# Gated cross-attention and FFN on one core: TensorE's blocks in another order, with the other engines' orders fitted to it

## The reference

```python
x = x + jnp.tanh(g_xattn[0]) * _L0_xattn_ref(_layernorm(x), ctx_1024, mask, Wq, bq, Wk, bk, Wo, bo)
x = x + jnp.tanh(g_ffn[0]) * _L0_ffn_ref(_layernorm(x), weights, scale, bias)

# _L0_xattn_ref, one head
Q = query @ Wq.T + bq;  K = ctx @ Wk.T + bk
attn = softmax(where(mask, -inf, Q @ K^T));  out = (attn @ ctx) @ Wo.T + bo
# _L0_ffn_ref
y = clip((x @ (2 * (weights >= 0) - 1).T) * scale + bias, -100, 100)
```

## Time and profile before

| | us |
|---|---|
| median of 3 runs | 83.87 (83.54 to 83.89) |
| the profiled execution | 83.47 |
| its span, first to last instruction | 81.3 |
| busy in the span: TensorE | 69.5 (85%) |
| VectorE, GpSimd | 55.1, 54.9 (68% each) |
| ScalarE | 36.5 (45%) |

### The profile page before, as it was taken

How to read it: one execution, slowest core, us unless ns; L and a number is a source line. 1 busy time by engine, 2 the same in 40 slices (tenths; PEclk the granted TensorE clock), 3 DMA queues, 4 the chain that set the end, 5 groups by cost and what they waited for, 6 DMA issues and landing times.

```text
span 81.3 us, 1571 instructions
## 1 busy us (share of the span) xinstructions
PE 69.5 (85%) x524; PEld 65.2 (80%) x524; DVE 55.1 (68%) x162; ACT 36.5 (45%) x98; POOL 54.9 (68%) x102
## 2 busy tenths in 40 slices
PE   2999899979999999999999999999999898905000
PEld 2998797967899999999999999999999797704000
DVE  2394823995369589939957962894697468972980
ACT  0052538736476519436751943585094436020000
POOL 6006557503898508889999998999998995149900
PEclk9999999999999999999999999999999999998555
DMA  1999999960000000030003003000300300300051
GB/s 16 274 371 353 349 347 348 348 186 0 0 4 0 0 0 8 0 133 0 0 23 110 8 0 129 0 0 0 129 8 0 129 0 0 129 0 0 0 194 65
DMA packets 7713, 7.44 MB, mean 92 GB/s; under 512 B 791, under 2 KB 7450, under 8 KB 7706
## 3 DMA queue, kind: packets, MB, share of 16 engines
q1 hardware_dynamic: 7376, 7.34, 28.0%
q10 hardware_dynamic: 330, 0.01, 0.2%
HBM read 5.25 MB, written 2.10 MB: 90 GB/s over the span
## 4 chain that ended last, share of the span: by engine, by line
PE 73%; DVE 14%; ACT 5%; issue 2%; POOL 2%; POOLq 0%; DVEq 0%; ACTq 0%
PE ps_K L514 16%; PE ps_Z L514 13%; PE ps_S L578 8%; PE ps_O L597 8%; PE ps_F L514 7%; PE ps_x1T L616 6%; PE ps_cT L509 4%; PE ps_xT L509 4%; PE ps_x1T L509 4%; ACT K_sb L205 2%; PE ps_S L586 2%; DVE cT_lo L372 2%; DVE out_sb L425 2%; DVE f_last L422 1%; DVE f_scaled L417 1%
## 5 line engine op out<-in xcount | busy, mean ns | idle before, releaser
L397 DVE SCALAR_TENSOR_TENSOR x_sb<-ps_O,recip_p,xb_sb 128x256 f32<-128x256 f32 x16 | 7.0, 479 | 10.4 <-PE ps_O L597 10.3
L314 POOL TENSOR_TENSOR f_biased<-f_scaled,bi_g 128x256 f32<-128x256 f32 x14 | 10.0, 735 | 3.8 <-DVE f_scaled L405 3.7
L308 POOL TENSOR_TENSOR xb_sb<-x_sb,bo_g 128x256 f32<-128x256 f32 x16 | 11.4, 733 | 0.5 <-ACT bo_g L241 0.5
L514 PE MATMUL ps_F<-wT,x1T_hi 128*128 128x256 f32 x32 | 8.6, 303 | 2.4 <-DVE f_scaled L405 2.3
L195 ACT CAST cT_hi<-ps_cT 128x512 fp32r<-128x512 f32 x8 | 4.7, 586 | 13.3 <-PE ps_cT L509 13.2
L296 POOL TENSOR_SCALAR xn<-x_sb,rstd_x,off_x 128x256 f32<-128x256 f32 x16 | 9.8, 621 | 0.5
L514 PE MATMUL ps_K<-cT_hi,wqk_hi 128*128 128x256 f32 x32 | 9.3, 290 | 0.9 <-DVE cT_lo L372 0.9
L514 PE MATMUL ps_Z<-woT_hi,cT_hi 128*128 128x256 f32 x32 | 9.7, 304 | 0.0
L514 PE MATMUL ps_K<-cT_hi,wqk_lo 128*128 128x256 f32 x32 | 9.0, 282 | 0.0
L514 PE MATMUL ps_K<-cT_lo,wqk_hi 128*128 128x256 f32 x32 | 9.0, 281 | 0.0
L514 PE MATMUL ps_Z<-woT_lo,cT_hi 128*128 128x256 f32 x32 | 9.0, 280 | 0.0
(11 more groups left out here) (102 smaller groups left out, 195.0 us busy)
## 6 DMA issues: line engine op xcount, KB each, us to landing
x_sb<-in_x_dram SPq DMA_DIRECT2D x8, 256.0 KB, 5.9
ctx_sb<-in_ctx_dram SPq DMA_DIRECT2D x8, 256.0 KB, 6.1
out_dram<-out_sb SPq DMA_DIRECT2D x7, 256.0 KB, 2.1
wq_sb<-in_L_xattn_Wq_dram SPq DMA_DIRECT2D x1, 256.0 KB, 3.1
wk_sb<-in_L_xattn_Wk_dram SPq DMA_DIRECT2D x1, 256.0 KB, 3.4
wo_sb<-in_L_xattn_Wo_dram SPq DMA_DIRECT2D x1, 256.0 KB, 4.5
w_sb<-in_L_ffn_weights_dram SPq DMA_DIRECT2D x1, 256.0 KB, 4.9
out_dram<-out_sb SPq DMA_DIRECT2D x2, 128.0 KB, 1.9
```

The costliest lines, as they stand in the source:

```text
L308: nc.gpsimd.tensor_tensor(xb_sb[:, r], x_sb[:, r], bo_g[:], ALU.add).then_inc(xb_done, 1)
L314: nc.gpsimd.tensor_tensor(f_biased[:, r], f_scaled[:, r], bi_g[:], ALU.add).then_inc(f_biased_done, 1)
L397: nc.vector.scalar_tensor_tensor(out=x1_sb[:, r], in0=ps_O[:, b], scalar=recip_p[:, r:r + 1], in1=xb_sb[:, r], op0=ALU.mult, op1=ALU.add). ...
L514: last = nc.tensor.matmul(dst, lhsT, rhs, start=(n == 0), stop=(n == len(pairs) - 1))
```

## The change

TensorE's loop becomes, for iteration i: Z(i), K(i+1), ffn(i-1), P^T(i), transposes of ctx(i+2) and x(i+2), O(i), scores(i+1), transposes of x1(i). scores(0) and the transposes of group 1 stand ahead of the loop. The orders on ScalarE, VectorE and GpSimd change with it, and the second unit of four rows of x is cut in two units of two. No computation is added or taken away, except that GpSimd computes one more unit's offsets (four small instructions).

```diff
--- before.py
+++ after.py
@@ -40,9 +40,9 @@
     row = lambda v: v.rearrange("(o d) -> o d", o=1)
 
 
-    UNITS = [(0, 2), (2, 4), (4, 8), (8, 12), (12, 16)]
-
-    STATS_AT = {0: (2, 3), 1: (4, 5), 2: (6,), 3: (7,)}
+    UNITS = [(0, 2), (2, 4), (4, 6), (6, 8), (8, 12), (12, 16)]
+
+    STATS_AT = {1: (4, 5), 2: (6,), 3: (7,)}
     unit_of = lambda g: next(n for n, (lo, hi) in enumerate(UNITS) if lo <= g * GB < hi)
 
     with ExitStack() as stack:
@@ -239,26 +239,31 @@
             nc.scalar.activation(woT_hi[:], ps_woT, ACT.Identity, scale=tanh_g[:, 0:1]).then_inc(woT_hi_ready, 1)
             act.wait_ge(ps_bo_ready, 1)
             nc.scalar.activation(bo_g[:], x1T_bank[:, 0:D], ACT.Identity, scale=tanh_g[:, 0:1]).then_inc(bo_g_ready, 1)
+            evict_cT_hi(1)
+            exp(0)
+            evict_xT(1)
             for i in range(G - 1):
-                evict_cT_hi(i + 1)
-                exp(i)
                 if i >= 1:
                     evict_x1T_hi(i - 1)
-                evict_xT(i + 1)
+                    exp(i)
                 evict_Z(i)
-                evict_PT(i)
                 evict_K(i + 1)
                 if i == 0:
                     act.wait_ge(ps_wT_ready, 1)
                     nc.scalar.copy(wT[:], ps_x1T).then_inc(wT_ready, 1)
+                evict_PT(i)
+                if i + 2 < G:
+                    evict_cT_hi(i + 2)
+                    evict_xT(i + 2)
+                if i == 0:
                     act.wait_ge(ps_rows_ready, 1)
                     nc.scalar.activation(sc_g[:], f_bank[:, 0:D], ACT.Identity, scale=tanh_g[:, 1:2]).then_inc(sc_g_ready, 1)
                     nc.scalar.activation(bi_g[:], f_bank[:, D:2 * D], ACT.Identity, scale=tanh_g[:, 1:2]
                                          ).then_inc(bi_g_ready, 1)
             exp(G - 1)
+            evict_x1T_hi(G - 2)
             evict_Z(G - 1)
             evict_PT(G - 1)
-            evict_x1T_hi(G - 2)
             evict_x1T_hi(G - 1)
 
         @block.gpsimd
@@ -325,21 +330,20 @@
             norm_x(1)
             pool.wait_ge(bo_g_ready, 1)
             for i in range(G):
-                add_bo(i)
-                if i == 2:
-                    pool.wait_ge(bi_g_ready, 1)
-                    pool.wait_ge(clip_ready, 2)
-                if i >= 2:
-                    bias_and_clip(i - 2)
+                if i >= 1:
+                    rstd_1s(i - 1)
                 if i + 2 < G:
                     if unit_of(i + 2) != unit_of(i + 1):
                         offsets_x(unit_of(i + 2))
                     norm_x(i + 2)
+                add_bo(i)
+                if i == 1:
+                    pool.wait_ge(bi_g_ready, 1)
+                    pool.wait_ge(clip_ready, 2)
                 if i >= 1:
-                    rstd_1s(i - 1)
-
+                    bias_and_clip(i - 1)
             rstd_1s(G - 1)
-            bias_and_clip(G - 2)
+
             for b in range(GB):
                 r = (G - 2) * GB + b
                 pool.wait_ge(f_clip_done, G - 1)
@@ -462,42 +466,38 @@
             dve.wait_ge(abs_g_done, 1)
             nc.vector.tensor_scalar(clip_hi[:], abs_g[:], CLIP, None, ALU.mult).then_inc(clip_ready, 1)
             nc.vector.tensor_scalar(clip_lo[:], abs_g[:], -CLIP, None, ALU.mult).then_inc(clip_ready, 1)
-            for i in range(G - 1):
-                if i >= 1:
-                    residual(i - 1)
-                max_of_scores(i)
-                if i >= 2:
-                    scale_ffn_out(i - 2)
-                if i == 0:
-                    dve.wait_ge(w_loaded, 16)
-                    nc.vector.tensor_scalar(w_sign2[:], w_sb[:], 0.0, 2.0, ALU.is_ge, ALU.mult).then_inc(sign2_done, 1)
-                    dve.wait_ge(sign2_done, 1)
-                    nc.vector.tensor_reduce(w_sum[:], w_sign2[:], AX.X, ALU.add).then_inc(w_sum_done, 1)
-                split_cT(i + 1)
-                if i == 0:
-                    dve.wait_ge(w_sum_done, 1)
-                    nc.vector.tensor_scalar(w_mean[:], w_sum[:], 1.0 / D, None, ALU.mult).then_inc(w_mean_done, 1)
-                    dve.wait_ge(w_mean_done, 1)
-                    for c in range(DC):
-                        nc.vector.tensor_scalar(w_cent[:, c], w_sign2[:, c], w_mean[:, c:c + 1], None, ALU.subtract
-                                                ).then_inc(w_cent_ready, 1)
+            max_of_scores(0)
+            split_cT(1)
+            stats_x(2)
+            dve.wait_ge(w_loaded, 16)
+            nc.vector.tensor_scalar(w_sign2[:], w_sb[:], 0.0, 2.0, ALU.is_ge, ALU.mult).then_inc(sign2_done, 1)
+            dve.wait_ge(sign2_done, 1)
+            nc.vector.tensor_reduce(w_sum[:], w_sign2[:], AX.X, ALU.add).then_inc(w_sum_done, 1)
+            dve.wait_ge(w_sum_done, 1)
+            nc.vector.tensor_scalar(w_mean[:], w_sum[:], 1.0 / D, None, ALU.mult).then_inc(w_mean_done, 1)
+            dve.wait_ge(w_mean_done, 1)
+            for c in range(DC):
+                nc.vector.tensor_scalar(w_cent[:, c], w_sign2[:, c], w_mean[:, c:c + 1], None, ALU.subtract
+                                        ).then_inc(w_cent_ready, 1)
+            stats_x(3)
+            for i in range(G):
                 if i >= 1:
                     stats_x1(i - 1)
                     split_x1T(i - 1)
+                if i >= 2:
+                    final(i - 2)
                 for g in STATS_AT.get(i, ()):
                     stats_x(g)
-                if i >= 2:
-                    final(i - 2)
-            scale_ffn_out(G - 3)
-            max_of_scores(G - 1)
-            residual(G - 2)
-            stats_x1(G - 2)
-            final(G - 3)
-            split_x1T(G - 2)
+                if i >= 1:
+                    scale_ffn_out(i - 1)
+                if i + 2 < G:
+                    split_cT(i + 2)
+                if i < G - 1:
+                    residual(i)
+                    max_of_scores(i + 1)
             residual(G - 1)
             stats_x1(G - 1)
             split_x1T(G - 1)
-            scale_ffn_out(G - 2)
             last_group()
 
         @block.tensor
@@ -631,34 +631,38 @@
             transposes(ps_woT, wo_sb).then_inc(ps_woT_ready, 1)
             pe.wait_ge(rows_loaded, 48)
             nc.tensor.matmul(x1T_bank[:, 0:D], ones_1[:], bo_row[:], start=True, stop=True).then_inc(ps_bo_ready, 1)
+            scores(0)
+            transpose_ctx(1)
+            transpose_x(1)
             for i in range(G - 1):
-                scores(i)
-                transpose_ctx(i + 1)
-                if i >= 1:
-                    transpose_x1(i - 1)
-                transpose_x(i + 1)
+
                 project_Z(i)
                 project_K(i + 1)
-                transpose_p(i)
                 if i == 0:
                     pe.wait_ge(bo_g_ready, 1)
                     pe.wait_ge(w_cent_ready, DC)
                     transposes(ps_x1T, w_cent).then_inc(ps_wT_ready, 1)
+                else:
+                    ffn(i - 1)
+
+                transpose_p(i)
+                if i == 0:
                     pe.wait_ge(woT_lo_ready, 1)
                     nc.tensor.matmul(f_bank[:, 0:D], ones_1[:], sc_row[:], start=True, stop=True)
                     nc.tensor.matmul(f_bank[:, D:2 * D], ones_1[:], bi_row[:], start=True, stop=True).then_inc(ps_rows_ready, 1)
-                else:
-                    ffn(i - 1)
-                if i == G - 2:
-                    scores(G - 1)
+                if i + 2 < G:
+                    transpose_ctx(i + 2)
+                    transpose_x(i + 2)
                 attend(i)
+                scores(i + 1)
+                transpose_x1(i)
             project_Z(G - 1)
             transpose_p(G - 1)
-            transpose_x1(G - 2)
+            ffn(G - 2)
             attend(G - 1)
-            ffn(G - 2)
             transpose_x1(G - 1)
             ffn(G - 1)
+
 
 
 # ---- launch: one core; inputs and outputs as the reference has them ----
```

## The result

| | before | changed |
|---|---|---|
| median | 83.71 us (4 runs, 83.46 to 83.89) | 87.64 us (4 runs, 86.60 to 89.25) |
| ratio | | 1.043, 95% interval 1.033 to 1.054 |
| beside the first experiments | 83.56 (11 runs) | 87.65 (6 runs, 86.57 to 87.98), ratio 1.042 (1.036 to 1.049) |

A forecast was written before the change was run, and what follows sets the result against it. TensorE's work, 7.20 us per iteration, was taken as the bound. Start 0.8, five periods 3.55 and end 0.8 gave +5.15 on the profiled 83.47, so 88.6, stated as 88.7; range 86.9 to 90.0.

The forecast's parts named there:

- x1 transposes behind the scores: TensorE's loop: only the scores now cover the residual, so TensorE waits 0.45 us per iteration, period 7.65.
- the 0.40 from the residual's end to TensorE's normal time: Assumed 0.40 us from a VectorE instruction's end until the waiting TensorE block counts its normal time.
- Rival (b): Stalled x1 transposes start like unbroken ones; eight waits shrink by 0.2 us each, giving 87.1; chance 0.13.
- GpSimd's order: rstd of x1(i-1) and offsets stand ahead of xn(i+2); x transposes 0.40 to 0.45 us late in iterations 2 and 4.
- VectorE and GpSimd at the same time: VectorE's final add holds GpSimd's ve_x on their shared port: 0.25 us each in iterations 2 and 4.
- behind F(7) nothing is changed: Program's end: the work after the last group's F block was said to stay as before.
- The start: K(1) comes earlier but TensorE idles 1.2 us for w_cent; Z(1) starts 0.8 us later than before.
- The end: From Z(6) to F(7)'s end takes 0.8 us longer, F(7) now held by its split.
- Rival (a): TensorE's clock falls to half before F(7), which then costs 0.95 us more: 89.6; chance 0.22.
- Rival (c): Faster: passages between plain and rounded products are what costs; at 0.8 us each, 83.1 to 83.4; chance 0.04.
- Rival (d): The waits don't add up; only start and end remain, time within 0.5% of before; chance 0.03.
- The sign: Whole kernel: slower was given 0.93, same 0.03, faster 0.04.

The follow-up runs named there:

- the first experiments: First set of follow-up runs, mostly variants of the changed kernel; timed beside them, the kernel before took 83.56 us and the changed kernel, run again, 87.65 us.

## Why the prediction was right, point by point

The measured 87.64 lies in the range of 86.9 to 90.0, 1.1 below the 88.7. The terms:

**x1 transposes behind the scores.** Right in mechanism, too large: 0.45 was said, 0.26 to 0.28 was measured (7.46 against 7.20, and 7.18 with the wait covered). The step that failed is the 0.40 from the residual's end to TensorE's normal time. Measured are 0.05 to the weight load and 0.22 of restart, 0.27. I had taken the 0.14 from f_scaled before F(7), and read the 0.14 ahead of the weight load in the earlier trace rows as a price of the wait; there TensorE's own row of work set it. The 0.14 ahead of F(7) appears again in the run of the kernel before with GpSimd held back, and ahead of the w_cent transposes (18.31 to 18.44), but not at the x1 transposes. Why these differ stays open. With 0.27 in place of 0.45 in each of eight waits, 1.4 us of the forecast falls away, more than its whole excess. Rival (b) priced this at 0.2 per wait and 87.1 in all, which is nearly the size that came; its mechanism, a stalled block that starts like an unbroken one, did not hold, since the block still lost 0.22.

**GpSimd's order.** Right in place: xn was waited for in iterations 2 and 4, as one row per iteration of the chain shows. The size was 0.40 to 0.45 there and at most 0.1 in iteration 1; measured above the 7.46 are 0.70 and 0.34. A shorter wait for x1 brings the ctx transposes' end nearer to the statistics, so the wait for xn grows by what the other loses: 0.18 more on each would make 0.28 and 0.63. The two terms hide one another, as the run with the x1 transposes inside Z also showed, where iteration 1 kept its 7.81.

**VectorE and GpSimd at the same time.** The mechanism is real (0.64 in place of 0.19 in a variant), but it cost little where I priced it. In iteration 2 of the changed kernel (timeline):

```profile
32.75 0.70 POOL L308 TENSOR_TENSOR rstd<-ve,half 128x2 f32<-128x2 f32 x1
33.03 0.68 DVE L414 TENSOR_TENSOR out_sb<-f_clip,x_sb 128x512 f32<-128x512 f32 x1
33.54 0.23 POOL L286 TENSOR_SCALAR ve_x<-mv_x 128x4 f32<-128x4 f32 x1
```

The add had 0.17 left when ve_x started, since the x1 transposes were earlier than I had them, and ve_x lost 0.04; in iteration 4 it lost 0.05. So the 0.5 counted for it is 0.1. The Trainium skill's page "SBUF — State Buffer", section "SBUF: two separate sides", gives the instruction that starts first the ports for its whole length. For ve_x both cases agree with it. The three rows above don't: rstd had started 0.28 ahead of the add and ran on until 33.45, and the add still took its usual 0.68; there the measurement decides. The page would also have pointed at a place that I missed: VectorE's last group in the kernel before, two instructions of which lost 0.67 to GpSimd. (The final add there has two SBUF inputs, as the page asks; f_last has one, and no run here shows whether the page's rule takes it in.) The prediction said that behind F(7) nothing is changed. That step was wrong, by -0.69.

**The start.** 0.8 was said, 0.61 measured; K(1) earlier and w_cent late as described. **The end.** 0.8 was said; 16.52 - 15.03 - 0.87 = 0.62 without the clock. Rival (a), the clock's fall before F(7), priced at +0.95, was given a chance of 0.22. By the two levels of the times it came in about four executions of six; one of them is traced, at 0.87, and filling the gaps took 1.05 off the median. It was a part of the measured median, not a rival to it.

**Rival (c)** is refuted: 0.01 per passage at most. **Rival (d)** didn't occur.

So the sum came out near in part by luck: one missed gain (-0.69), two terms too large (-1.4 and -0.4) and two too small (xn +0.9, the clock +0.9) partly cancel, and the traced execution's shorter warm-up (-0.42) has nothing to do with the change. The sign rested on the waits for the residual and xn, and each was shown by a run that removed it alone or nearly alone.

## What to carry to other kernels

Where one engine's work fills every iteration, moving a block of it pays only at the ends; before moving, compare what now lies between a result and its reader with the time that the other engine needs, and look at the queue ahead of that reader too. On the engines beside it, work that waits for the newest result belongs behind work that waits for nothing: GpSimd's offsets and xn cost nothing once they stood ahead of rstd, though its load was the same. It has to fit, though: with x + bo and the offsets of the same iteration put ahead of rstd as well, f_scaled became late. And when two waits lie behind one another, removing one shows nothing until the other is gone.

## What the runs showed of the hardware

Products in float32r next to plain float32 ones cost next to nothing for the passage: 0.01 us each at most, in iterations without idle time.

TensorE's granted clock fell from 2.4 to 1.2 GHz after gaps of 1.2 and 1.4 us with one block of 0.66 us between them, and eight products then took 2.09 in place of 1.22. It did so in some executions only: in four of nine traces with the same gaps the products ran at the full clock. Constant transposes in those gaps held up nothing, and with them four of six executions were at the lower level of the times, against two of six without.

A short GpSimd instruction (0.19) that starts during VectorE's add of two SBUF tensors ends with it (0.64 and 0.69 with most of the add left, 0.23 with 0.17 of it left). A GpSimd rstd that was already running didn't hold the add. The other way round, VectorE's last instructions took 0.70 and 0.82 in place of 0.42 while GpSimd added two 128x256 tiles.
